# First cross attention of a decoder: column groups for the variance sums, an output product in high and low parts, sums and scalings on DVE

## The reference

```python
def proj(t):
    x = layer_norm(t, ln_g, ln_b) @ w_in.T              # 256 -> 1024
    return x.reshape(Qd, Nd, H, D).transpose(2, 0, 1, 3)  # 8 heads of 128
f_q, f_k, f_v = proj(q), proj(k), proj(v)               # k = v = the context
cosine_sim = dots / (qn[..., :, None] * kn[..., None, :])
q_ratio = 2.0 * jnp.minimum(q_var, 1.0) / (q_var + 1.0)
k_ratio = 2.0 * jnp.minimum(k_var, 1.0) / (k_var + 1.0)
var_component = jnp.einsum('hqn,hqm->hqnm', q_ratio, k_ratio)
cov_component = cosine_sim * decorr_scale
mixed = cw * cosine_sim + vw * cov_component + ww * var_component
out = jnp.einsum('hqnm,hqmd->hqnd', mixed, f_v)
return out.transpose(...).reshape(...) @ w_out.T + b_out
```

## Time and profile before

| | us |
|---|---|
| median of three runs | 3550.13 (3542.46 to 3554.76) |
| the profiled execution | 3530.47, its span 3528.7 |
| the stage of the change, third step | from 405 to 976 |
| PE, weight loads, DVE, ACT busy in the whole span | 2860.3, 2200.3, 1824.1, 1206.1 |
| mean granted clock of PE in the span | 0.892 of 2.4 GHz |

### The profile page before, as it was taken

The page is one execution under the profiler, slowest core; times in us unless marked ns, Lnnn a source line. Parts: engine busy times, 40 slices in busy tenths (PEclk is TensorE's granted clock), DMA queues, the critical chain, the costliest instruction groups (busy, mean ns, idle before and its releaser), DMA issues. The chain is left out here.

```text
span 3528.7 us, 55915 instructions
## 1 busy us (share of the span) xinstructions
PE 2860.3 (81%) x17893; PEld 2200.3 (62%) x17894; DVE 1824.1 (52%) x4037; ACT 1206.1 (34%) x3124; POOL 501.0 (14%) x408
## 2 busy tenths in 40 slices
PE   3877699999963899999707999999996979965397
PEld 3766477777752577777505777777775956644263
DVE  4554477777534122222265666666666567745323
ACT  1330133433330111111134555555543456640021
POOL 0000000000006000000152333233333001100303
PEclk9998699999965899999858999999998989985696
DMA  7000000000035111111131000000000733324364
GB/s 277 0 0 2 0 1 0 0 0 0 0 96 185 35 33 33 33 33 33 43 88 36 1 1 0 0 0 0 0 0 19 232 97 88 90 75 136 120 182 128
DMA packets 165353, 184.96 MB, mean 52 GB/s; under 512 B 22208, under 2 KB 152464, under 8 KB 163728
## 3 DMA queue, kind: packets, MB, share of 16 engines
q1 hardware_dynamic: 136464, 144.86, 13.3%
q0 software_dynamic: 9216, 25.18, 2.2%
q10 hardware_dynamic: 19584, 13.79, 1.2%
HBM read 115.57 MB, written 68.19 MB: 52 GB/s over the span
## 5 line engine op out<-in xcount | busy, mean ns | idle before, releaser
L1459 ACT ACTIVATE a_prob<-a_s_ps,a_ntop 128x256 f32<-128x256 f32 x512 | 235.6, 472 | 356.1 <-DVE a_ntop L1533 356.1
L1508 POOL TENSOR_TENSOR a_prob<-a_prob,a_rden 128x1024 f32<-128x1024 f32 x128 | 242.4, 1894 | 604.3 <-DVE a_rden L1538 604.3
L2651 PE MATMUL e0x_up_ps<-e0w_upT,e0x_xgT 128*128 x576 | 263.4, 600 | 0.8 <-ACT e0x_xgT L2694 0.6
L2669 PE MATMUL e0x_y_ps<-e0w_downT,e0x_hT 128*128 x1152 | 260.5, 379 | 1.0 <-DVE e0x_hT L2710 1.0
L2717 DVE COPY e0x_y<-e0x_y_ps 128x256 f32<-128x256 f32 x72 | 30.5, 424 | 438.8 <-PE e0x_y_ps L2669 438.8
L2669 PEld LDWEIGHTS e0x_y_ps<-e0w_downT,e0x_hT 128*128 128x128 f32 x1152 | 218.8, 190 | 61.3 <-issue 35.2
L2125 DVE TENSOR_REDUCE x1a_top<-x1a_s_ps 128x4 f32<-128x1024 f32 x128 | 155.9, 1222 | 71.5 <-PE x1a_s_ps L1986 69.7
L2071 ACT ACTIVATE x1a_prob<-x1a_st_ps,x1a_mask_now 128x512 f32<-128x512 f32 x256 | 162.3, 686 | 88.8 <-PE x1a_st_ps L2002 86.6
L1533 DVE TENSOR_REDUCE a_ntop<-a_s_ps 128x4 f32<-128x1024 f32 x128 | 156.3, 1221 | 68.2 <-PE a_s_ps L1384 68.2
L2651 PEld LDWEIGHTS e0x_up_ps<-e0w_upT,e0x_xgT 128*128 128x128 f32 x576 | 104.1, 191 | 106.2 <-issue 105.8
L2697 ACT ACTIVATE e0x_h<-e0x_up_ps 128x512 f32<-128x512 f32 x144 | 86.0, 597 | 243.7 <-PE e0x_up_ps L2651 243.7
(11 more groups left out here) (539 smaller groups left out, 7198.4 us busy)
## 6 DMA issues: line engine op xcount, KB each, us to landing
x_qk<-head_rows SPq DMA_DIRECT2D x384, 64.0 KB
head_rows<-x1p_rows_out SPq DMA_DIRECT2D x32, 512.0 KB, 3.7
e1w_ew<-in_L_ffn_expert_w_dram SPq DMA_DIRECT2D x8, 2048.0 KB, 17.9
sorted_tokens<-zeros SPq DMA_DIRECT2D x12, 1024.0 KB, 21.1
e1x_xg<-sorted_tokens SPq DMA_DIRECT2D x96, 128.0 KB, 2.3
sorted_results<-e1x_y ACTq DMA_DIRECT2D x96, 128.0 KB, 2.4
e0x_xg<-sorted_tokens SPq DMA_DIRECT2D x72, 128.0 KB, 2.0
sorted_results<-e0x_y SPq DMA_DIRECT2D x72, 128.0 KB, 1.7
```

What stands on the lines that cost most here:

```text
L1459: last = act.activation(prob[:, h % RING, n, t, :], s_ps[:, n, t * SEQ:(t + 1) * SEQ], ACT.Exp, bias=ntop[:, h % RING, n, t:t + 1], accum_ ...
L1508: last = pool.tensor_tensor(p, p, scale_of, ALU.mult)
L2651: last = pe.matmul(up_ps[half][:], xgT[:, p, k, :], upT[:, bass.ds(e, 1), k, half * 512:(half + 1) * 512].rearrange("p a d -> p (a d)"), s ...
L2669: last = pe.matmul(y_ps[p][:, 0:DIM], hT[:, p, c, :], downT[:, bass.ds(e, 1), c, :].rearrange("p a d -> p (a d)"), start=c == 0, stop=c == ...
```

## The change

- T is laid out in four groups of 32 columns: s_diag has 32 columns per head, head 2j+i goes to column i of group j, and its products write partitions 32j to 32j+31. T, t_sb and rT now have 128 partitions; the ratios of the queries are written to a zeroed tile, spread, with a group's two heads every 34 columns, before R transposes them. ww becomes a column over 128 partitions, made by a small product with a zeroed tile, place.
- O is computed in fp32r from high and low parts of gT and b_sb: three products for each one before. ACT copies the high part of each G and B bank (two heads in one copy), DVE subtracts it for the low part, and only that frees the bank.
- c1 is no longer applied to B by ACT but to the keys' reciprocal norms by DVE (`scale`), before g.
- The sums of f and of its squares are taken for each of the four tiles, one tile behind the F banks. sq has two tiles instead of four, g one buffer instead of two.
- In DVE's turn the order is now: F banks with the sums, the low parts of G, B, G, X and Y (`turned`), then the small steps and scalings, then the output. G's first transposes wait for the scaled queries on their own; ACT takes the square root before T.
- The parts wg are made in the mixing step, at its start on ACT and after `bc` on DVE.

```diff
@@ l0_cross_mixing
+                pe.matmul(bank[4][:, 2 * XH:2 * XH + 1], place[:, 0:P], wts[:, 2:3], start=True, stop=True)
...
             def _(act):
+                act.copy(wg[0][:], wgT[:]).then_inc(s_high, 1)
...
+                dve.memset(place[:], 0.0).then_inc(s_one, 1)
+                dve.wait_ge(s_one, 3)
+                dve.tensor_copy(place[:].rearrange("p (j c) -> p j c", c=VAR_STEP)[:, :, 0:2],
+                                sh.ident[0:XH, 0:XH].rearrange("p (j i) -> p j i", i=2))
...
+                dve.wait_ge(s_high, 1)
+                dve.tensor_tensor(wg[1][:], wgT[:], wg[0][:], ALU.subtract)
...
+                dve.tensor_copy(ww[:], bank[4][:, 2 * XH:2 * XH + 1])
@@ l0_cross_batches, tensor
                     elif kind == "T":
                         pe.wait_ge(drained["A"], 3 * (b + 1))
-                        for h in range(XH):
-                            last = pe.matmul(o[0:XH, 0:DIM], s_diag[:, h, :], woT[:, h, :], start=h == 0, stop=h == XH - 1)
+                        for i in range(2):
+                            for j in range(VAR_GROUPS):
+                                last = pe.matmul(o[32 * j:32 * (j + 1), 0:DIM], s_diag[:, 2 * j + i, :], woT[:, 2 * j + i, :],
+                                                 start=i == 0, stop=i == 1)
...
                     elif kind == "G":
+                        if n == 0:
+                            pe.wait_ge(s_q, TPB * (b + 1))
...
                             for h in range(XH):
-                                pe.matmul(o[:, t * DIM:(t + 1) * DIM], gT[:, h, t * P:(t + 1) * P], b_sb[:, h, :],
-                                          start=h == 0, stop=False)
+                                for n, (x, y) in enumerate(HIGH_LOW):
+                                    pe.matmul(o[:, t * DIM:(t + 1) * DIM], gT[x][:, h, t * P:(t + 1) * P], b_sb[y][:, h, :],
+                                              start=h == 0 and n == 0, stop=False)
@@ l0_cross_batches, scalar
                 def front(b, p):
-                    wait_past(act, s_fsq, b)
                     for side in range(SIDES):
+                        wait_past(act, s_fsq, SIDES * b + side - 1)
                         act.wait_ge(drained["F"], 8 * b + 2 * side + 2)
-                        act.activation(sq[:, side, :], f[:, p, side, :], ACT.Square).then_inc(s_sq, 1)
+                        act.activation(sq[:, side % 2, :], f[:, p, side, :], ACT.Square).then_inc(s_sq, 1)
...
                     turned(b, 0)
                     turned(b, 1)
+                    if after is not None:
+                        norms(after)
...
                     for n in range(4):
                         act.wait_ge(filled["B"], 4 * b + n + 1)
-                        for i in range(2):
-                            h = 2 * n + i
-                            last = act.activation(b_sb[:, h, :], bank[place[("B", n)]][:, i * DIM:(i + 1) * DIM], ACT.Copy,
-                                                  scale=c1[:, h:h + 1])
-                        last.then_inc(drained["B"], 1)
-                    if after is not None:
-                        norms(after)
+                        act.copy(b_sb[0][:, 2 * n:2 * n + 2, :].rearrange("p h d -> p (h d)"), bank[place[("B", n)]][:]).then_inc(
+                            high["B"], 1)
@@ l0_cross_batches, vector
+                def squares(b, p, side):
+                    dve.wait_ge(drained["F"], 8 * b + 2 * side + 2)
+                    dve.tensor_reduce(fsum[:, side, :], f[:, p, side, :].rearrange("p (h d) -> p h d", d=HD),
+                                      AXIS.X, ALU.add).then_inc(s_side, 1)
+                    dve.wait_ge(s_sq, SIDES * b + side + 1)
+                    dve.tensor_reduce(fsq[:, side, :], sq[:, side % 2, :].rearrange("p (h d) -> p h d", d=HD), AXIS.X,
+                                      ALU.add).then_inc(s_fsq, 1)
...
+                        if half == 1 and side > 0:
+                            squares(b, p, side - 1)
+                    squares(b, p, SIDES - 1)
...
+                    step.then(dve.tensor_tensor(rnorm[:, 0:TPB, :], rnorm[:, 0:TPB, :],
+                                                c1[:].unsqueeze(1).broadcast_to([P, TPB, XH]), ALU.mult))
...
+                def low(kind, dst, b, n):
+                    dve.wait_ge(high[kind], 4 * b + n + 1)
+                    part = [a[:, 2 * n:2 * n + 2, :].rearrange("p h d -> p (h d)") for a in dst]
+                    dve.tensor_tensor(part[1], bank[place[(kind, n)]][:], part[0], ALU.subtract).then_inc(drained[kind], 1)
+
+                def turned(b):
+                    for n in range(2):
+                        low("G", gT, b, n)
+                    for n in range(4):
+                        low("B", b_sb, b, n)
+                    for n in range(2, 4):
+                        low("G", gT, b, n)
+                    tokens(b + 2)
...
+                def turn(b, p):
+                    step = Steps(dve, s_f, (b + 1) * F_STEPS)
+                    front(b + 1, 1 - p)
+                    turned(b)
+                    scale(b + 1, 1 - p, step)
+                    back(b, p)
```

More of the change, by code:

```diff
@@ L150, in __init__ @@
         self.out_bias = sb(cross, "x0_out_bias", [P, DIM])
-        self.wgT = sb(cross, "x0_wgT", [P, KC, INNER])
+        self.wg = [cross.enter_context(nc.sbuf_tensor(f"early_x0_wg_{part}", [P, KC, INNER], F32R)) for part in ("high", "low")]
+        self.c1 = sb(cross, "x0_c1", [P, XH])
+        self.ww = sb(cross, "x0_ww", [P, 1])
         self.woT = sb(cross, "x0_woT", [P, XH, DIM])
         self.fbias = sb(cross, "x0_fbias", [P, INNER])
+        self.wgT = sb(weights, "x0_wgT", [P, KC, INNER])
         self.w_nat = sb(weights, "x0_w_nat", [P, XH, DIM])
@@ L985, in _ @@
                 pool.memset(s_diag[:], 0.0).then_inc(s_zero, 1)
+                pool.memset(spread[:], 0.0).then_inc(s_zero, 1)
             @block.tensor
@@ L1033, in job @@
                         for t in range(TPB):
-                            last = pe.transpose(o[0:XH, t * P:(t + 1) * P], ratio[:, p, TPB + t, :], sh.ident[:])
+                            last = pe.transpose(o[:, t * P:(t + 1) * P], spread[:, p, t, 0:P], sh.ident[:])
                     elif kind == "O":
@@ L1123, in back @@
                     tokens(b + 2)
[L1125 to L1126 removed]
+                act.wait_ge(s_zero, 2)
                 tokens(0)
```

110 lines of the change are left out of this document (52 added, 58 removed).

## The result

The changed kernel takes 3528.58 us (median, 3526.3 to 3532.24) against 3550.66 of the kernel before (3542.46 to 3555.45), six runs of each. The ratio is 0.9939, with a 95% interval of 0.9926 to 0.9952: 22 us faster. The prediction said 3541, 9 faster; the measured time lies outside its own range (3534 to 3550) and inside the one that takes in the rivals (3512 to 3570).

The account below looks back on a forecast made before the run. PE bounds the kernel before, DVE after. Start 7.0, turns 15.2 and end 5.6, less 0.7 for mixing, save 27; clock falls take 18, so 3550.1 - 9 = 3541 us. Own range 3534 to 3550, with rivals 3512 to 3570.

Parts of the forecast that it names:

- PE's part: PE's work per turn: T saves 2.5, O 1.8, the tail products 0.4, from 33.5 to 28.8 us.
- DVE becomes the bound: DVE's work per turn rises from 26.2 to 31.8 us, mostly eight low parts (4.8), above PE's 28.8.
- The gap before T: PE stands still about 3.7 us before T, from 9.8 to 13.6 of DVE's turn.
- The turn without the clock: A steady turn takes 32.6 us against 33.5, saving 0.9; bounds 32.2 and 33.3.
- The clock: PE's clock falls on T, R and B, costing 1.5 in 12 of 14 turns: 18 us lost.
- rival 1: PE's clock holds through the gap before T: 27 saved, 3523 us; chance 0.25.
- The start: Stage start: first batch out 7 us earlier by sums beside products and early weights' parts; mixing step pays 0.7.
- The end: Last batch of the stage: DVE's wait for PE's chain of products shortens by 5.6 us.
- Rival 2: On B, the clock falls longer or twice a turn: stage 12 us longer, 3562; chance 0.20.
- Rival 3: DVE's bound is higher, 33.3 us a turn, with the clock up: 17 saved, 3533; chance 0.10.
- Rival 4: T's column groups don't run side by side, T stays 3.55: 10 us slower, 3560; chance 0.05.

Follow-up runs that it names:

- fill3: The changed kernel with three extra products written into T's bank ahead of T's wait for the A banks: 3521.41 us, ratio 0.9915.
- gap2: The changed kernel with one more ACT copy of 2048 columns per turn ahead of the A banks: 3578.6 us in one run.
- The last kernel: The changed kernel with O in fp32, whole-batch sums (pieces for batch 0 only), root behind B banks, scalings ahead of the tokens: 3497.39 us, ratio 0.9852.
- gap1: The changed kernel with one more ACT copy of 1024 columns per turn ahead of the A banks: 3557.4 us in one run.
- the filler above: The changed kernel with six extra products written into T's bank ahead of T's wait for the A banks: 3513.69 us, ratio 0.9961.
- a_first: The changed kernel with ACT copying the three A banks before it squares the fourth tile: 3517.79 us, ratio 0.9901.

## Why the prediction was right, and where its sizes were wrong

The direction held, and so did the main mechanism, that DVE becomes the bound and PE gets a gap before T. The number of falls didn't hold, and the gain was 2.5 times the forecast. By its own steps:

**PE's part: right.** T fell from 3.55 to 1.00 (1.05 taken). The fp32r products of O start 0.12 apart (0.113 taken), the halves take 2.93 and 3.05 us against 3.62 in fp32, so O saved 1.3 and not 1.8. A tail takes 0.25 instead of 0.62, so both saved 0.7 where 0.4 was counted. PE's work in a turn is 32.25 - 2.17 - 0.90 = 29.2 (28.8 said). With the column groups alone a turn fell by 3.3, for T and the tails 2.9 had been counted.

**DVE becomes the bound: right.** Busy 32.23 of 34 us, that is 30.6 in a turn of 32.25 (30 to 31 said). The sums of a quarter follow each other every 1.13 (1.14 taken), the low parts every 0.60 to 0.65.

**The gap before T: mis-sized.** 3.7 said, 1.4 to 2.2 found. Two ends of it were off. T started 13.04 us into DVE's turn (652.74 - 639.70) instead of 13.6: the last F bank was drained at 10.7, not 11.0, and the copies up to T took 1.4, not 1.5. And PE had ended its G banks at 10.9, not at 9.8. F started 5.1 ahead of DVE's turn (634.57), not 5.5: O ended 27.1 us into the turn, as laid out, but the turn was shorter. And F, A and the two G banks took 16.0 us where the layout had 15.3.

**The turn without the clock: mis-sized.** 32.6 said, with 32.2 as the lower bound; 31.8 and 32.2, mean 32.0, found (fill3 shows it for all turns). B came earlier by the same 0.6, and DVE stood for 0.5 at the B banks (0.21, and 2.69 for four instead of 2.40) where 0.8 had been laid out. Fourteen turns without a fall save 24.0 (469.5 before, 445.5 in fill3) where 15.2 was said: 8.8 more.

**The clock: right in its kind and its price, wrong in its number.** The price of a fall on T is 1.6, 1.5 was said. But 4 of 14 turns had one, and one more had it on O, not 12, so the loss in them is 7.5 (24.0 - 16.5) instead of 18, and the granted clock of the stage is 0.96, not near 0.93. Nine of the fourteen turns ran at 1.00, which the prediction had named as the sign of rival 1. The step that failed is the one before it, the gap: gap2 has the gap that was predicted, and there the clock falls in every turn. By the sentence from the Trainium skill, TensorE: Matmul & The Clock Gate, section Part 4: PE-mode transpose, all 14 would fall. In the kernel after they don't: every gap before T stands behind the same two G banks of transposes, and ten of fourteen passed at full clock. But 14 was worked out for a gap of 3.7, and in gap2, which has that gap, all fourteen fall; whether the transposes count is settled by neither.

**The start: the size right, its cause only in part.** 6.3 said (7.0 less 0.7), 5.5 found: from the first normalisation to the first output the kernel before takes 73.4 us and the kernel after 67.4, and the normalisation comes 0.5 later. The prediction put it down to the sums beside F and the early weights. But the column groups alone, which have neither, take 69.7, so T and the tails give 3.7 of the 6.0 by themselves. The last kernel, which adds the sums and the weights to them, gives 2.7 more; the change without the column groups (the old T) takes 69.6. That the size came out is partly luck.

**The end: too good.** 5.6 said, 2.2 found (22.64 to 20.40). Some 1.5 us of the difference are a fall of the clock on O, at 939, for which DVE waits. The kernel with the sums over the whole batch has the same chain of products in its last turn, without a fall:

```profile
966.00:972.00 6.00, 4.08 (x33) 3.83 (x31) 1.89 (x3) 0.94 (x2) 0.00 (x0) 1.00 0.00 0
```

There half of O with its tail takes 3.20 us (968.14 to 971.34) against 4.68, and the last turn 18.91. Without the fall the end would thus save 3.7. What is left of the 5.6 is the 0.9 of the turns' difference, which isn't in this chain, and the low parts of G, for which PE waits 1.93 ahead of O where it waited 1.22 before (at 962.75). The kernels with O in fp32 have a last turn of 19.1, so that O in parts neither wins nor loses there.

The sum: 5.5 + 24.0 - 7.5 + 2.2 = 24.2 in the stage, and 22 in the medians. Against the forecast of 9, the turn gave 8.8 more and the clock took 10.5 less; the start and the end gave 0.8 and 3.4 less.

**The rivals.** Rival 1 (the clock holds, 3523) lies 6 from the outcome of 3528.6, the forecast 12: with a third of the falls that the forecast had, the truth is between the two, nearer to the rival. Rival 2 (slower by falls on B) has its mechanism shown in gap1 and gap2, but the kernel after has too few falls for it. (Its 3562 is a slip: 14 turns of 3.0 are 42, less 27 that is 15 longer, 3565.) Rival 3 (DVE's bound higher) is refuted by turns of 31.8. Rival 4 is refuted by T's 1.00 us.

**What the prediction did not ask.** It priced the parts and not whether each pays. It also called the sixteen records of an O half sixteen products; they are eight products of two records, which the sum for O did not feel, but the filler above did. And in the part on the change, head 2j+i has column 2j+i of its group, not column i; that is why its row is 34j+i and the ratios stand every 34 columns. By its own numbers O in parts saves 1.8 us on PE and adds 4.8 on DVE, and T alone would have left PE's turn at 33.5 - 2.5 - 0.4 = 30.6 with DVE at 26.2 and the small copies behind it. The Trainium skill, TensorEngine Tiling (Array Packing), section PSUM Bottleneck, was cited for the banks' emptying as the new limit; the runs narrow that. With the column groups alone the emptying keeps up with a turn of 30.25, and PE is busy 33.69 of 34. It became the limit by the work that the change itself added to it.

## What to carry to other kernels

When a change lightens one engine and loads another, price each of its parts alone against both engines: the one that saves on the bound and costs nothing elsewhere may be worth more than the whole. A gap on an engine that is no longer the bound costs little by itself (0.2 us a turn here), but a fall of the clock after it costs if what follows is awaited: 1.6 on T, 0.2 or less on O where O had slack. And before a count of clock falls is built on a gap, size the gap from both of its ends: 3.7 us said and at most 2.2 found was the difference between a fall in every turn and in four of fourteen.

## What the runs showed of the hardware

- A fall of PE's clock came after 4 of 13 gaps of 1.4 to 2.2 us in the kernel after, and at each of 26 gaps of 2.3 to 4.0 in gap1 and gap2. The length of the gap alone doesn't decide: there 2.17 passed and 2.07 didn't, and in the first attention of the kernel before two gaps of 2.6 passed (at 156 and 180). The falls of the kernel after lie 129 to 130 us apart from 587 on, every fourth turn, those of a_first (the A banks first) 96 apart, every third, and those of the sums over the whole batch 34.1 apart, every turn. What sets this wasn't tried.
- The same gap of 2.41 us before O brought a fall in each of twelve turns of one kernel (the sums over the whole batch, which also has 0.89 us of idle time ahead of its second G banks) and in three of seven of another (the A banks first). This stays open too.
- Six dead products of two records each, 0.44 us a product, kept the clock at 1.00 in all steady turns; so did three, 1.3 us of a gap of 2.2.
- A short spell at the lower level loses 1.7 us of PE's time (0.57 over the four microseconds from 587, 0.66 over the five from 938), and costs between nothing and 1.6 us of the turn, by where it lies.
